# K's bias on VectorE, a new order of TensorE's step end, and value rows made once

## The reference, cut to what matters

```python
h = layernorm(x) * (1 + ca) + sa
Q = elu(h @ Wq + bq) + 1;  K = elu(h @ Wk + bk) + 1;  V = h @ Wv + bv
out = einsum(Q, einsum(K, V)) / (einsum(Q, K.sum) + 1e-6)       # per head
x1 = layernorm(h + out @ Wo + bo) * g1 + beta1
z  = layernorm(x1 + relu(x1 @ W1 + b1) @ W2 + b2) * g2 + beta2
x2 = x + ga * z
h2 = layernorm(x2) * (1 + cb) + sb
xr, xk = mu * h2 + (1 - mu) * h2_of_the_row_before              # two mixes
result = x2 + gb * sigmoid(xr @ W_r) * (relu(xk @ W_k)**2 @ W_v)
```

## Time and profile before

| | |
|---|---|
| median of 3 runs | 162.54 us (162.42 to 162.72) |
| the profiled execution, its time | 162.81 us |
| its span, first to last instruction | 160.7 us |
| granted TensorE clock | 1.0 of full speed in the whole span |
| PE, DVE, ACT, POOL busy | 97%, 77%, 79%, 65% |
| chain that ended last | PE 93%, DMA 2%, DVE 2%, ACT 1% |

### The profile page before, as it was taken

How to read it: one execution, slowest core, us unless ns; L and a number is a source line. 1 busy time by engine, 2 the same in 40 slices (tenths; PEclk the granted TensorE clock), 3 DMA queues, 4 the chain that set the end, 5 groups by cost and what they waited for, 6 DMA issues and landing times.

```text
span 160.7 us, 4111 instructions
## 1 busy us (share of the span) xinstructions
PE 155.6 (97%) x1151; PEld 145.1 (90%) x1151; DVE 123.1 (77%) x572; ACT 127.3 (79%) x346; POOL 104.6 (65%) x243
## 2 busy tenths in 40 slices
PE   7899999999999999999999999999999999999992
PEld 6778998999999999999999999999999999888891
DVE  3766878597887969696978779796969777888842
ACT  4256777889797979898997979797989989656562
POOL 4337567576676767787676767676877755973631
PEclk9999999999999999999999999999999999999999
DMA  4926299920010101010100101010101001010112
GB/s 122 269 90 174 67 276 369 423 115 0 2 37 0 33 0 33 4 37 0 34 5 0 33 4 35 0 35 4 33 0 35 4 0 33 2 37 0 35 33 67
DMA packets 8974, 9.94 MB, mean 62 GB/s; under 512 B 724, under 2 KB 7416, under 8 KB 8952
## 3 DMA queue, kind: packets, MB, share of 16 engines
q1 hardware_dynamic: 8656, 9.60, 18.8%
q10 hardware_dynamic: 296, 0.08, 0.2%
HBM read 7.55 MB, written 2.13 MB: 60 GB/s over the span
## 4 chain that ended last, share of the span: by engine, by line
PE 93%; DMA 2%; DVE 2%; ACT 1%; issue 0%; SPq 0%; DVEq 0%
PE bank L1266 16%; PE bank L1156 16%; PE bank L1145 8%; PE bank L1238 5%; PE bank L1194 5%; PE bank L1150 5%; PE bank L1222 4%; PE bank L1182 4%; PE bank L1230 4%; PE bank L1378 4%; PE bank L1210 4%; PE bank L1206 4%; PE bank L1249 3%; DMA kqvo<-in_kqvo 2%; PE bank L1219 1%; PE bank L1398 1%
## 5 line engine op out<-in xcount | busy, mean ns | idle before, releaser
L1156 PE MATMUL bank<-w,hid 128*128 128x128 f32 x240 | 31.7, 275 | 0.0
L1266 PE MATMUL bank<-x1T,w 128*128 128x256 f32 x120 | 30.9, 381 | 0.0
L1156 PEld LDWEIGHTS bank<-w,hid 128*128 128x128 f32 x240 | 29.3, 192 | 0.0
L347 ACT ACTIVATE hid<-bank,b_cols 128x256 f32<-128x256 f32 x60 | 26.0, 511 | 1.1 <-PE bank L1266 1.1
L544 POOL TENSOR_TENSOR rstd_n<-vare_n,power 128x2 f32<-128x2 f32 x30 | 23.8, 792 | 2.4
L1266 PEld LDWEIGHTS bank<-x1T,w 128*128 128x128 f32 x120 | 21.5, 190 | 2.7 <-DVE z L803 0.2
L710 DVE TENSOR_SCALAR ny<-bank,mv_ny,rstd_ny 128x128 f32<-128x128 f32 x32 | 11.7, 406 | 9.0 <-POOL rstd_ny L544 9.0
L323 ACT ACTIVATE hT<-bank,modT 128x256 f32<-128x256 f32 x16 | 9.0, 565 | 11.3 <-PE bank L1145 11.3
L540 POOL TENSOR_TENSOR vare_n<-mv_n,eps 128x2 f32<-128x2 f32 x30 | 5.9, 195 | 17.2 <-DVE mv_n L704 17.1
L292 ACT ACTIVATE n<-x_all,shift_n,rstd_n 128x128 f32<-128x128 f32 x27 | 11.8, 485 | 2.5 <-POOL shift_n L552 2.5
L317 ACT ACTIVATE keepT<-bank,modT 128x255 f32<-128x255 f32 x26 | 13.1, 555 | 0.0
(11 more groups left out here) (187 smaller groups left out, 454.7 us busy)
## 6 DMA issues: line engine op xcount, KB each, us to landing
gm_rows<-mod_rows_dram SPq DMA_DIRECT2D x2, 960.0 KB, 9.5
out<-out_sb SPq DMA_DIRECT2D x15, 128.0 KB, 1.8
gm_rows<-mod_rows_dram SPq DMA_DIRECT2D x1, 768.0 KB, 6.7
w<-in_w SPq DMA_DIRECT2D x1, 512.0 KB, 5.6
x_all<-in_x SPq DMA_DIRECT2D x1, 512.0 KB, 5.6
bv_row<-bv_rows_dram SPq DMA_DIRECT2D x1, 512.0 KB, 7.1
bv_row<-bv_rows_dram SPq DMA_DIRECT2D x1, 384.0 KB, 4.4
gm_rows<-mod_rows_dram SPq DMA_DIRECT2D x1, 384.0 KB, 3.7
```

Source lines behind the costliest of these rows:

```text
L347: last = nc.scalar.activation(hid[:, f, :], bank[:, f % 2 * L:(f % 2 + 1) * L], ACT.Relu, bias=b1_cols[:, f:f + 1])
L1156: last = nc.tensor.matmul(banks[6][:, c * D:(c + 1) * D], hid[:, f, c * 128:(c + 1) * 128], w2[:, f, :], start=False, stop=(f == FF - 1 an ...
L1266: return nc.tensor.matmul(bank[:, f % 2 * L:(f % 2 + 1) * L], w1[:, f * 128:(f + 1) * 128], x1T[:, :], start=True, stop=True)
```

## The change

1. K's bias. The bf16 matmul of each step goes. VectorE instead adds the bias row (`bias_rows`, float32, on all partitions) to K on its way out of `bank4`: a new operation per sample, `k_biased`, which writes `kb` in SBUF. `exp_k` and `k_elu` read `kb`. Sample 0 keeps a matmul, now one float32 matmul with the identity.
2. TensorE's step end. n1's transposes of the next sample move from the head of the step to right behind z's last product; the mix's value product, which stood in the middle of z's sums, moves behind them, so z's products are one run.
3. n1's statistics and `first_scale` run a step earlier, with two buffers for `rstd_n1` and `shift_n1`.
4. VectorE's order in a step: z's `mv` ahead of `gated`, `centred` ahead of the denominators, the two `mix_half` apart from each other, with `k_elu` and `middle` between.
5. The opening: the row of the value bias is made once for all samples (`bv_product`, then `bv_rows`) and `direct_row` picks a row of it; n1 of sample 0 is turned without its shift, which `hT` adds; three matmuls that only kept TensorE busy go; the order in the opening changes on all engines.

The diff, cut to its core (the buffers, semaphores and constants are left out):

```diff
             def k_exponent(s):
-                need(act, k_mm, s + 1)
-                nc.scalar.activation(exp_k[:, :, :], chunked(banks[4]), ACT.Exp, bias=neg1[:, :]).then_inc(expk_ok, 1)
+                if s == 0:
+                    act.wait_ge(k_mm, 1)
+                need(act, kb_ok, s)
+                source = kb[:, :, :] if s else chunked(banks[4])
+                nc.scalar.activation(exp_k[:, :, :], source, ACT.Exp, bias=neg1[:, :]).then_inc(expk_ok, 1)
...
             def k_elu(s):
                 need(dve, expk_ok, s + 1)
-                nc.vector.scalar_tensor_tensor(k_sb[:, :, :], exp_k[:, :, :], 1.0, chunked(banks[4]), ALU.min,
-                                               ALU.max).then_inc(k_ok, 1)
+                plain = kb[:, :, :] if s else chunked(banks[4])
+                nc.vector.scalar_tensor_tensor(k_sb[:, :, :], exp_k[:, :, :], 1.0, plain, ALU.min, ALU.max).then_inc(k_ok, 1)
+
+            def k_biased(s):
+                need(dve, k_mm, s + 1)
+                need(dve, bias_rows_ok, 1)
+                nc.vector.tensor_tensor(kb[:, :, :], chunked(banks[4]), bias_rows[:, :].unsqueeze(1).broadcast_to([128, NC, D]),
+                                        ALU.add).then_inc(kb_ok, 1)
...
             def k_product(s):
+                if s == 0:
+                    pe.wait_ge(bias_rows_ok, 1)
+                    nc.tensor.matmul(chunked(banks[4]), ident[:, :], bias_rows[:, :].unsqueeze(1).broadcast_to([128, NC, D]),
+                                     start=True, stop=False)
+                    bv_product()
+                elif s == 1:
+                    pe.wait_ge(k_ok, 1)
                 need(pe, hT_ok, s + 1)
-                need(pe, k_ok, s)
+                need(pe, kb_ok, s - 1)
                 need(pe, tanh_ok, s - 4)
-                nc.tensor.matmul(chunked(banks[4]), ones3[:, :], bias_parts[:, :].unsqueeze(1).broadcast_to([128, NC, D]),
-                                 start=True, stop=False)
...
             def direct_row(s):
-                pe.wait_ge(cols_ok, 3)
-                pe.wait_ge(wvo_loaded, 16)
-                pe.wait_ge(bv_loaded, 16)
-                dest = banks[2][:, s * D:(s + 1) * D]
-                nc.tensor.matmul(dest, modT[:, ROW, s:s + 1].broadcast_to([128, 128]), wv, start=True, stop=False)
-                nc.tensor.matmul(dest, part128[:, :], bv_pad[:, :], start=False, stop=True).then_inc(direct_mm, 1)
+                pe.wait_ge(bv_ok, 1)
+                nc.tensor.matmul(banks[2][:, s * D:(s + 1) * D], ident[0:S, s:s + 1].broadcast_to([S, 128]), bv_rows[:, :],
+                                 start=True, stop=True).then_inc(direct_mm, 1)
...
# TensorE, step(t), its end
-                if live(t):
-                    value_of_state(sa)
-                feed_forward_out(0, 2)
...
+                if t == 3:
+                    feed_forward_out(0, 2)
+                    value_of_state(sa)
+                    need(pe, hidb_ok, sd + 1)
                 else:
-                    feed_forward_out(2, FF).then_inc(z_mm, 1)
+                    value_of_state(sa)
+                    feed_forward_out(0, 2)
+                feed_forward_out(2, FF).then_inc(z_mm, 1)
+                if live(t + 1):
+                    n1_transposes(sa + 1)
+                if live(t - 4):
+                    value_of_mix(sc)
...
# ScalarE, first_steps, sample 2
                 h_turned(2)
...
-                k_exponent(2)
                 q_exponent(2)
+                q_relu()
                 attention_turned(1)
                 x1_turned(0)
-                q_relu()
+                k_exponent(2)
...
# VectorE, first_steps, sample 2
                 y_norm(0)
+                k_biased(2)
...
                 k_elu(2)
+                q_elu(2)
                 x_stats(3)
                 x_mv(3)
                 y_stats(1)
                 norm_mv("ny", 2)
-                q_elu(2)
                 second_columns()
                 shift_columns()
                 y_norm(1)
                 masked_state(2)
+                x_stats(4)
+                x_mv(4)
...
# VectorE, step(t), steps 3 to 15 (step_end now takes z's mv before the gate)
+                    centred(sp_)
+                    denominators(sb_)
+                    reciprocals(sb_)
+                    k_biased(sa)
+                    attention(sb_)
+                    if live(t - 4):
+                        mix_half(K_W, sc)
+                    k_elu(sa)
+                    middle(sp_)
+                    need(dve, x2_ok, sp_ + 1)
+                    norm_stats("n3", lambda c: x2_p[:, c, :])
+                    if live(t - 4):
+                        mix_half(R_W, sc)
+                    norm_mv("n3", sp_ + 1)
+                    y_stats(sb_)
+                    q_elu(sa)
+                    norm_mv("ny", sb_ + 1)
+                    if live(t + 2):
+                        x_stats(t + 2)
+                        x_mv(t + 2)
+                    masked_state(sa)
+                    shift_of_n3(sp_)
+                    y_norm(sb_)
```

More of the change, by code:

```diff
@@ L76, in build @@
         bv_rows = sb("bv_rows", [S, D])
-        bias3 = sb("bias3", [3, D])
-        bias_k = sb("bias_k", [3, D])
-        part_mask = sb("part_mask", [3, 2])
-        high = [sb(f"high{i}", [3, D], BF16) for i in range(2)]
-        rest = sb("rest", [3, D])
-        bias_parts = sb("bias_parts", [128, D], BF16)
+        bias_rows, bv_bias = sb("bias_rows", [128, D]), sb("bv_bias", [S, D])
         x_all = sb("x_all", [128, S * NC, D])
@@ L96, in build @@
         wv_plus = [sb(f"wv_plus{p}", [128, D + H]) for p in range(2)]
-        mean_r, shift_n1, one_pair = (sb(n, [128, NC]) for n in ("mean_r", "shift_n1", "one_pair"))
+        mean_r, one_pair = (sb(n, [128, NC]) for n in ("mean_r", "one_pair"))
+        rstd_n1, shift_n1 = ([sb(f"{n}{p}", [128, NC]) for p in range(2)] for n in ("rstd_n1_", "shift_n1_"))
         kvs = sb("kvs", [128, D + H])
@@ L290, in take_n1 @@
                 wait_x(act, s)
-                for c in chunks:
-                    last = nc.scalar.activation(n1[s % 2][:, c, :], x_all[:, NC * s + c, :], ACT.Identity,
-                                                scale=rstd["n1"][:, c:c + 1], bias=shift_n1[:, c:c + 1])
+                for c in range(NC):
+                    last = n1_part(s, c)
                 last.then_inc(n1_ok, 1)
-            take_n1(0, (0,))
+            act.wait_ge(bias_mm, 1)
+            act.wait_ge(const_pool, 1)
+            nc.scalar.activation(bias_rows[:, :], banks[6][:, D:2 * D], ACT.Identity, scale=-1.0,
+                                 bias=one_pair[:, 0:1]).then_inc(bias_rows_ok, 1)
+            act.wait_ge(x_in[0], 16)
+            act.wait_ge(shift_n1_ok, 1)
+            n1_part(0, 0)
             act.wait_ge(cols_ok, 2)
@@ L360, in first_steps @@
             def first_steps():
-                h_turned(0)
+                act.wait_ge(hT_mm, 1)
+                nc.scalar.activation(hT[0][:, :], banks[0][:, 0:L], ACT.Identity, scale=mod_col(CA, 0),
+                                     bias=shift_first[:, :]).then_inc(hT_ok, 1)
+                n1_part(0, 1).then_inc(n1_ok, 1)
                 k_exponent(0)
@@ L907, in first_steps @@
                 reciprocals(0)
+                k_biased(1)
                 attention(0)
                 k_elu(1)
+                direct_weights(1)
                 need(dve, aks_mm, 1)
@@ L1366, in step @@
                     residual_into(banks[6], x1T, c)
-                if live(t):
-                    value_of_state(sa)
-                feed_forward_out(0, 2)
-                if t == 3:
-                    need(pe, hidb_ok, sd + 1)
-                if live(t - 4):
-                    need(pe, ksq_ok, sc + 1)
-                    need(pe, wvg_ok, sc + 1)
-                    need(pe, q_ok, sc + 5)
-                    need(pe, prod_ok, sc)
-                    for c in range(NC):
-                        last = nc.tensor.matmul(banks[5][:, c * D:(c + 1) * D], ksqT[:, c * 128:(c + 1) * 128], gate_tile(sc)[:, :],
-                                                start=True, stop=True)
-                    last.then_inc(v_mm, 1)
                 if draining(t):
+                    feed_forward_out(0, 2)
+                    value_of_mix(sc)
                     need(pe, hidb_ok, sd + 1)
@@ L1386, in step, with value_of_mix @@
                     feed_forward_out(3, FF).then_inc(z_mm, 1)
-                else:
-                    feed_forward_out(2, FF).then_inc(z_mm, 1)
+                    return
+                if t == 3:
+                    feed_forward_out(0, 2)
+                    value_of_state(sa)
+                    need(pe, hidb_ok, sd + 1)
+                else:
+                    value_of_state(sa)
+                    feed_forward_out(0, 2)
+                feed_forward_out(2, FF).then_inc(z_mm, 1)
+                if live(t + 1):
+                    n1_transposes(sa + 1)
```

(11 more changed lines are left out.)

203 lines of the change are left out of this document (84 added, 119 removed).

## The result

The kernel after takes 164.36 us (median of 14 runs, 164.16 to 164.82) against 162.78 us (14 runs, 162.42 to 163.94) of the kernel before beside it: ratio 1.0095, 95% interval 1.0079 to 1.0110. It is slower by 1.6 us. Its profiled execution took 164.4 us, with a span of 162.7; before, the span was 160.7. So 2.0 us are to be found in the spans of the two traces, 0.4 us more than between the medians. The traced execution of the kernel before is one of its shortest by span (160.7 us, where the 29 and 25 executions of it beside experiments 1 to 4 and 5 to 8 have medians of 161.2 and 161.1), and it has 2.1 us around its span, the traced one after 1.7.

The account below looks back on a forecast made before the run. TensorE, busy 97%, was taken to bound the kernel. Terms of +0.7 us (steps 4 to 15), 0 (z in one run) and +1.1 (opening) made +1.8 on a median of 162.54: 164.3 us, range 162.0 to 165.6.

Parts of the forecast that it names:

- rival A: Whole kernel: the terms as summed, 164.3 us, own range 163.4 to 165.2, chance 0.55.
- The bias matmul's 0.11 us: Steps 4 to 15: removing this matmul saves 0.11 us a step on PE alone, 1.3 us in all.
- attT ends later than PE: Steps 4 to 15, output product: PE arrives at +3.71 and must wait for ScalarE's attT, starting at +3.83.
- Rival B: Steps 4 to 15: the matmul time is simply gone, -1.3 us, opening's product in time; 160.5 us, chance 0.13.
- Its size: Steps 4 to 15: 0.12 us waiting and 0.05 restarting against 0.11 saved, +0.06 us a step.
- The term as a whole: Steps 4 to 15 together: 12 x 0.06 = +0.7 us, bounds -1.3 to +1.3.
- Step 4: Counted as one of the 12 equal steps 4 to 15, at +0.06 us like the rest.
- kb's cover: Steps: k_biased on VectorE has kb ready 0.3 us ahead of exp_k's turn on ScalarE, so it stays hidden.
- Rival E: Steps: k_biased comes 0.1 us beyond its cover, adding 1.2 us; 165.5 us, chance 0.12.
- Step 3 and part 2, both set to 0: Step 3: 0, between -0.4 and +0.3; z in one run with n1's transposes at its end: 0 in steps 4 to 15.
- The opening: Before the steps: PE waits for GpSimd's late wv_plus of sample 2, +1.1 us, bounds +0.8 and +1.4.
- the gain at x1T: Opening: the first x1T starts 0.45 us earlier, bounds 0.2 and 0.7.
- What would show it: Steps of 8.82 to 8.86 us, PE waiting for attT, falling busy share, over 1 us wait for wv_plus.

Follow-up runs that it names:

- experiments 1 to 4 and 5 to 8: Two groups of follow-up kernels, each kernel run beside the kernel before for comparison.
- experiment 5: Kernel after with sample 3's n1 statistics first, attT ahead of the first hid, and K's bias a bf16 TensorE matmul in samples 1 to 15: 162.23 us.
- experiment 10: Kernel after with sample 3's n1 statistics first, attT ahead of the first hid, and the biased K written back into PSUM: 160.63 us.
- kernel of both edits: Kernel after with n1's statistics of sample 3 ahead of sample 2's k_sb and qT, and attT ahead of the first hid: 161.01 us.
- Experiment 2: Kernel after with ScalarE making attT ahead of the first hid in every step: 162.43 us.
- experiment 6: Kernel before with ScalarE making attT ahead of the first hid: 163.17 us, ratio 1.0019.
- experiment 8: Kernel after with sample 3's n1 statistics first and the biased K written back into its PSUM bank instead of SBUF: 162.60 us.
- experiment 9: The kernel of both edits with sample 5's statistics moved from step 3 into step 4, behind the first mix half: 166.54 us.
- Experiment 7: The kernel of both edits with the mix's value product moved back between z's sums: 161.54 us.
- experiment 1: Kernel after with VectorE taking n1's statistics and mv of sample 3 ahead of k_sb and qT of sample 2 in the opening: 162.97 us.

## Why the prediction was right

The forecast was 164.3 us for rival A, the measured median 164.36. So close a hit is partly luck: the forecast of +1.8 us was added to a median of three runs, 162.54, where the fourteen runs beside the change have 162.78 and give +1.6; and between the traces it is +2.0, 0.3 us more than forecast in the opening, 0.1 less in steps 4 to 15. Point by point:

- **The bias matmul's 0.11 us.** Right, in size too: 8.77 to 8.66 (experiments 5 and 10), and in their rows K's product starts 1.04 and 0.93 us after the attention product. The 0.08 to 0.10 that the kernel of both edits shows is less by its wait for k_sb.
- **attT ends later than PE.** Right. Experiment 2 takes it away and the step falls by 0.13; experiment 6 shows that it was no wait before. Rival B would have had 8.67 us a step; that is what the change brings once ScalarE's order is changed too (8.69, and 8.66 with K in PSUM).
- **Its size.** +0.06 us a step was too much: it is +0.03 in steps 5 to 14, and the step of 8.81 us lies just under the 8.82 to 8.86 that I had named as the sign. The output product started at +3.80 from ny's transposes, where I had +3.83. The adder of exp_k was 0.04 instead of 0.05 (experiment 8), the hand-over 0.05 instead of 0.06, and the restart 0.05 as taken. So PE loses 0.09 by waiting (3.71 to 3.80) and 0.05 by restarting, for the 0.11 saved. The term as a whole, +0.7 for steps 4 to 15, still met its sum (0.36 + 0.25 + 0.03 = 0.64), because step 4 lost 0.36 alone. That agreement is luck.
- **Step 4.** This was mis-sized, as one of twelve equal steps. Before, it was 0.01 us longer than the later ones; after, it is 0.34 longer, and with attT first still 0.23. So 0.11 goes by attT's lateness, which experiment 2 shows, as it shows step 3 shorter by 0.23, more than a step's 0.13. The rest can be read in the rows. In the kernel after K's product in step 4 starts 1.14 us after the attention product (33.70), 0.93 in the later steps, since hT stands on ScalarE behind n3, which waits for VectorE:

```profile
33.46 0.88 ACT L451 ACTIVATE n<-x,shift_n,rstd_n 128x128 f32<-128x128 f32 x2 [0.69 <-DVE shift_n L789]
...
34.84 0.71 PE L1228 MATMUL bank<-kqvo,hT 128*128 128x128 f32 x4
```

The same in the kernel of both edits, step 4:

```profile
32.35 0.55 ACT L327 ACTIVATE hT<-bank,modT 128x256 f32<-128x256 f32 x1
...
32.95 0.71 PE L1228 MATMUL bank<-kqvo,hT 128*128 128x128 f32 x4
...
33.50 0.60 PE L1236 MATMUL bank<-hT,kqvo 128*128 128x256 f32 x2
```

hT ends 0.05 us before K's product, and Q's product starts 1.56 us after the attention product (31.94), 1.38 in the later steps: 0.18 us. The rest is k_sb's, 0.59 us long there. Experiment 10, without k_sb's part, is 0.18 longer in step 4 than later. That is read from rows; no edit took hT's lateness away, and experiment 9 did not get to it.

- **kb's cover.** Right: 0.3 us forecast, 0.37 measured. Rival E did not come. Experiment 7 shows that the cover comes from part 2: with z's end back where it was, kb is late for exp_k.
- **Step 3 and part 2, both set to 0.** Step 3 came out at -0.04 us, with exp_k waiting 1.01 us for kb there, as I had it. For the later steps it is not shown in this kernel; experiment 7 gives part 2 0.03 us a step where attT is early; what it is worth where attT is late is only estimated there. Leaving it at 0 overlooked that part 2 makes kb's cover.
- **The opening.** Right in mechanism (experiment 1 gives all of it back), +1.40 us against +1.1. From x1T's start to mv_n's end it is 2.54 us, forecast 2.56. From there to the product 3.08, forecast 2.99. From the product to the attention product 1.43, as before. What was mis-sized is the gain at x1T: 19.23 to 19.05, 0.18 us, below the 0.2 that I had as its lower bound, not 0.45, though K's first product came 0.47 us sooner (7.79 to 7.32). I had charged `k_biased` on samples 1 and 2 for what is lost on that way. In the rows of sample 1 it does stand between K's product and the state's (2.16 us from start to start, 1.63 before). But experiment 5, which has no `k_biased`, starts the first x1T at 19.04, 11.85 us after K's first product, and the kernel of both edits 11.74 after. So taking it away gives nothing back there; what ends last instead stays open.
- **What would show it.** Step length, ScalarE without a gap, PE waiting over 1 us for wv_plus, VectorE 1.1 us for exp_k: seen. Two signs were badly chosen. From step 4 on, the waits of PE for attT appear in no list of waits, and PE's busy share within a step did not fall.

## What to carry to other kernels

Before a matmul is moved off a bound TensorE, measure the distance from the end of the next thing TensorE waits for to the place where TensorE needs it; here it was 0.10 us for a matmul of 0.11, so nothing was left to gain until ScalarE's order was changed with it. And when a producer moves in one engine's queue, walk all queues behind it: in the opening, two operations on VectorE ahead of a statistic cost 1.4 us on TensorE by way of GpSimd, and in experiment 9 a statistic put off by one step cost 5.8. A null result of an edit (the order of ScalarE in experiment 6) says only that something else ends last there; it may be worth its time once that is gone. A step of equal length in every repetition can still hold a small wait that another engine's timing makes, as k_sb's in experiment 10: compare the rows of two kernels before a small difference is called noise.
